# Second layer's prologue: first x from the residual's buffer, mask cast in two halves, second head's parts built inside unit 0

## The reference, cut to what matters

```python
h = maximum(layernorm(x), 0)
q = (h @ W).reshape(B, N, 4, 64)
e_src, e_dst = q @ a[:64], q @ a[64:]          # one number per node and head
e = leaky_relu(e_src[:, :, None] + e_dst[:, None], 0.2)
attn = softmax(where(adj > 0, e, -9e15), axis=2)
x = x + elu(attn @ q)
```

## Time and profile before

| | us |
|---|---|
| median of 3 runs | 5178.77 (5178.1 to 5178.99) |
| the profiled execution | 5176.52 |
| its span | 5174.7 |

### The profile page before, as it was taken

One profiled execution on the slowest core, in us unless ns is written; L12 is line 12 of the kernel. 1 busy time (PEld: TensorE's weight loads), 2 busy tenths in 40 slices (PEclk: granted clock), 3 DMA queues, 4 the chain that ended last, 5 costly groups with the idle time before them and its releaser, 6 DMA issues. The chain is left out here.

```text
span 5174.7 us, 139408 instructions
## 1 busy us (share of the span) xinstructions
PE 4889.2 (94%) x56608; PEld 4437.5 (86%) x56608; DVE 3751.2 (72%) x7147; ACT 2886.9 (56%) x3121; POOL 1364.6 (26%) x1472
## 2 busy tenths in 40 slices
PE   6999999999999999999999999993989989989999
PEld 5988888888898888888988889983989988989899
DVE  6666666666666666666666666664898898988898
ACT  4444444444444444444444444443878888878887
POOL 3343343334334333433433334331000000110100
PEclk9999999999999999999999999996999999999999
DMA  5000000000000000000000000003121121120210
GB/s 197 9 9 9 13 18 9 14 9 17 14 9 9 10 14 17 9 14 9 17 14 9 9 9 13 5 5 131 38 68 54 44 74 47 55 74 26 77 62 28
DMA packets 100064, 164.65 MB, mean 32 GB/s; under 512 B 5089, under 2 KB 91489, under 8 KB 92961
## 3 DMA queue, kind: packets, MB, share of 16 engines
q1 hardware_dynamic: 98464, 144.80, 8.4%
q0 software_dynamic: 896, 10.23, 0.5%
HBM read 112.79 MB, written 38.03 MB: 29 GB/s over the span
## 5 line engine op out<-in xcount | busy, mean ns | idle before, releaser
L551 PEld LDWEIGHTS outs<-v_s,probs 128*128 128x128 f32 x16384 | 1973.8, 192 | 81.7 <-issue 3.3
L551 PE MATMUL outs<-v_s,probs 128*128 128x128 f32 x16384 | 1984.0, 275 | 0.6 <-DVE probs L794 0.6
L654 ACT ACTIVATE slot<-slot,shift 128x1024 f32<-128x1024 f32 x1024 | 1111.3, 1088 | 1429.6 <-PE slot L541 1429.6
L794 DVE SCALAR_TENSOR_TENSOR probs<-slot,bound 128x1024 f32<-128x1024 f32 x1024 | 1250.9, 1224 | 723.1 <-ACT slot L654 720.1
L1354 ACT ACTIVATE cond<-s_all,d_sign 128x1024 bf16<-128x1024 f32 x1024 | 1123.7, 1142 | 196.9 <-DVE u L1509 191.7
L387 POOL TENSOR_TENSOR ctx_sum<-ctx_sum,ctx_part 128x256 f32<-128x256 f32 x896 | 646.6, 728 | 1267.3 <-DVE ctx_part L810 1266.5
L540 PE MATMUL slot<-q_hi,k_hl 128*128 128x512 f32 x2048 | 902.1, 441 | 1.0 <-DVE q_lo L750 1.0
L1255 PE MATMUL sums<-x_mixed,u 128*128 128x130 f16 x8192 | 807.1, 222 | 0.0
L1509 DVE TENSOR_TENSOR u<-cond,mask 128x1024 f16<-128x1024 bf16 x1024 | 694.6, 686 | 152.0 <-PE sums L1259 78.0
L541 PE MATMUL slot<-q_lo,k_hl 128*128 128x512 f32 x2048 | 802.1, 392 | 0.0
L1259 PE MATMUL sums<-x_mixed,mask 128*128 128x65 f16 x8192 | 778.6, 196 | 0.0
(11 more groups left out here) (135 smaller groups left out, 3820.6 us busy)
## 6 DMA issues: line engine op xcount, KB each, us to landing
s_all<-s_turned SPq DMA_DIRECT2D x32, 1024.0 KB, 4.9
xs<-in_x SPq DMA_DIRECT2D x32, 512.0 KB, 4.9
x<-y SPq DMA_DIRECT2D x32, 512.0 KB, 3.3
x_s<-x SPq DMA_DIRECT2D x32, 512.0 KB, 4.8
o_s<-x SPq DMA_DIRECT2D x16, 1024.0 KB, 6.1
out<-o_s SPq DMA_DIRECT2D x16, 1024.0 KB, 5.5
probs<-in_adj SPq DMA_DIRECT2D x11, 1024.0 KB, 5.3
bound<-in_adj SPq DMA_DIRECT2D x5, 1024.0 KB, 4.9
```

The source lines that it names most:

```text
L551: end = nc.tensor.matmul(outs[i % OUTS][:, q, :], probs[:, i % PROBS, r, q * P:(q + 1) * P], v_s[:, c * JC + r, h * E1:h * E1 + P], start= ...
L654: nc.scalar.activation(slot[:, :, :], slot[:, :, :], ACT.Exp, bias=shift[:, 0:1], scale=SCALE).then_inc(act_done, 1)
L794: nc.vector.scalar_tensor_tensor(probs[:, i % PROBS, :, :], spot(kind, "step", s, i)[:, :, :], P_LOW, bound[:, (i // H) % 2, :, :], ALU.ma ...
```

## The change

- SP loads x of batch 0 straight into `o_s`, in its two halves, as its first transfers after the weights; the four strip loads of batch 0 are gone. The statistics and normalize of batch 0 read `o_s`; normalize still writes `xs`, and from strip 2 on it waits until PE has transposed the strip that was in that buffer.
- The mask load leaves the head of POOL's stream. It now stands behind the constants and a wait on the second half of x, and it is two loads, one for each half of the columns. `inverse_std` for strip 0 stands behind both. DVE waits for a mask half at the start of unit 0 and of unit 1 of batch 0.
- `weigh`, `low` and `back` of head 1 of batch 0 move from the prologue into unit 0: `weigh` at steps 1 and 2, `low` at 6 and 7, `back` at 8; ACT's `high` of head 1 comes after `cond` of step 4.

```diff
-            def load_strip(pb, k, guard):
-                if guard:
-                    sp.wait_ge(pro_filled, t_use(pb, k, T_PAIRS - 1) - 2 * STRIP_PRO + 1)
+            def load_strip(pb, k):
+                sp.wait_ge(pro_filled, t_use(pb, k, T_PAIRS - 1) - 2 * STRIP_PRO + 1)
...
+            for half in range(HALVES):
+                load_res(0, half, False)
             for k in range(NS):
-                load_strip(0, k, k >= 2)
-                if k >= 2:
-                    store_s(0, k - 2)
-            store_s(0, NS - 2)
-            store_s(0, NS - 1)
+                store_s(0, k)
             spread_d(0)
             load_s(0, 0, False)
-
-            for half in range(HALVES):
-                load_res(0, half, False)
...
-            pool.dma_start(mask16[:, :, :], mask_dram).then_inc(mask_loaded, 16)
-            nc.gpsimd.memset(lift[:, :], LIFT)
...
+            pool.wait_ge(res_loaded[1], 16)
+            nc.gpsimd.memset(lift[:, :], LIFT)
+            for half in range(HALVES):
+                cols = slice(half * HALF, (half + 1) * HALF)
+                pool.dma_start(mask16[:, :, cols], mask_dram[:, :, cols]).then_inc(mask_loaded[half], 16)
...
             weights(0)
             high(0, 0, False)
-            high(0, 1, False)
...
+                        if first and m == 0 and j == 4:
+                            high(b, 1, False)
...
             def statistics(pb, k):
-                dve.wait_ge(x_loaded[k % 2], (pb * (NS // 2) + k // 2 + 1) * 16)
+                if isinstance(pb, int) and pb == 0:
+                    dve.wait_ge(res_loaded[k // 2], 16)
+                    src = o_s[:, k * IT:(k + 1) * IT, :]
+                else:
+                    dve.wait_ge(x_loaded[k % 2], ((pb - 1) * (NS // 2) + k // 2 + 1) * 16)
+                    src = xs[:, k % 2, :, :]
...
             def normalize(pb, k):
                 dve.wait_ge(rstd_done, pb * NS + k + 1)
+                src = xs[:, k % 2, :, :]
+                if isinstance(pb, int) and pb == 0:
+                    src = o_s[:, k * IT:(k + 1) * IT, :]
+                    if k >= 2:
+                        dve.wait_ge(pro_filled, t_use(0, k - 2, T_PAIRS - 1) + 1)
...
-            for h in range(2):
-                weigh(0, h, 0)
-                weigh(0, h, 1)
-                low(0, h, 0)
-                low(0, h, 1)
-                back(0, h)
-            dve.wait_ge(mask_loaded, 16)
+            weigh(0, 0, 0)
+            weigh(0, 0, 1)
+            low(0, 0, 0)
+            low(0, 0, 1)
+            back(0, 0)
...
+                    if first and m < HALVES:
+                        dve.wait_ge(mask_loaded[m], 16)
...
+                        if first and m == 0:
+                            if j in (1, 2):
+                                weigh(b, 1, j - 1)
+                            if j in (6, 7):
+                                low(b, 1, j - 6)
+                            if j == 8:
+                                back(b, 1)
```

More of the change, by code:

```diff
@@ L1022, in layer1_block @@
         ones_ready = sem("ones_ready")
-        mask_loaded = sem("mask_loaded")
+        mask_loaded = [sem("mask_loaded0"), sem("mask_loaded1")]
         x_loaded = [sem("x1_loaded0"), sem("x1_loaded1")]
@@ L1146, in batch @@
                     if m < NS and not last:
-                        load_strip(b + 1, m, True)
+                        load_strip(b + 1, m)
                     if m < HALVES and not first:
@@ L1428, in statistics @@
             def statistics(pb, k):
-                dve.wait_ge(x_loaded[k % 2], (pb * (NS // 2) + k // 2 + 1) * 16)
+                if isinstance(pb, int) and pb == 0:
[4 more added lines that the diff above has]
+                    src = xs[:, k % 2, :, :]
                 for t in range(IT):
-                    last = nc.vector.bn_stats(stats[:, t, :], xs[:, k % 2, t, :])
+                    last = nc.vector.bn_stats(stats[:, t, :], src[:, t, :])
                 last.then_inc(stats_done, 1)
@@ L1442, in normalize @@
                 dve.wait_ge(rstd_done, pb * NS + k + 1)
+                src = xs[:, k % 2, :, :]
[3 more added lines that the diff above has]
+                        dve.wait_ge(pro_filled, t_use(0, k - 2, T_PAIRS - 1) + 1)
                 for t in range(IT):
-                    last = nc.vector.tensor_scalar(xs[:, k % 2, t, :], xs[:, k % 2, t, :], moments[:, t, 0:1], rstd[:, t:t + 1],
+                    last = nc.vector.tensor_scalar(xs[:, k % 2, t, :], src[:, t, :], moments[:, t, 0:1], rstd[:, t:t + 1],
                                                    ALU.subtract, ALU.mult)
```

## The result

| | us |
|---|---|
| kernel before, median of 7 runs | 5178.1 (5174.12 to 5182.56) |
| changed kernel, median of 7 runs | 5160.92 (5153.08 to 5162.7) |
| ratio, with its 95% interval | 0.9965 (0.9956 to 0.9974) |
| profiled execution of the changed kernel, span | 5162.7, 5160.9 |

The change makes the kernel 17 us faster, a third of a per cent. The forecast was 5161.3. That agreement is partly luck: the stage up to unit 1 gained 3 us more than forecast, and the time after it gave back about as much. One of the executions of e8 further down ran at a granted clock of 0.842 and took 5604.86 us; its ratio leaves that one out.

The account below looks back on a forecast made before the run. At the layer seam DVE stands 16.84 us for a_s behind the mask, everything else behind DVE. Terms 11.4 + 0.6 + 7.27 - 1.75 = 17.5 us, taken from 5178.8, give 5161.3; range 5153.5 to 5169.

Parts of the forecast that it names:

- part 3: Strips of batch 0: still 5.85 us apart; small stores hardly feel the moved mask, 0 (0 to 2 us lost).
- Part 1: Seam start, x ahead of the mask: DVE folds at 3518.2, ready for strip 0's rstd 16.9 us earlier.
- Part 2: POOL before strip 0's rstd: x wait and two mask issues of 3.28 us leave 11.4 us gained (16.9 to -7).
- rival A: POOL's mask issues nearly free, about 0.6 us per half: rstd moves 16.9, total gain 23.0 us, 5155.8; chance 0.18.
- the likeliest case: The main forecast, with 3.28 us of POOL's time per mask half: 5157 to 5166, chance 0.60.
- Rivals B: POOL held back by the DMA engines at the mask issue, free between 3535 and 3547: 5168 to 5180; chance 0.12.
- D: At POOL's mask issue each run costs a fixed 6 ns or more: slower, 5191 at 9 ns; chance 0.05.
- Part 4: Spread through memory: faster without the residual's 2 MB just behind it in the queue, 0.6 us gained (0 to 1.3).
- Part 5: Head 1's parts moved into unit 0: first pick 7.27 us earlier, unit 0 longer by 1.75 (0 to 7.2).
- the walk: Stepping through unit 0 on the old clock: DVE waits 1.5 us for ACT's cond 5, later conds early.
- Rival C: Unit 0 starves PE, whose clock stays low longer, costing 5 to 8 us: 5168; chance 0.05.
- The lead should reach the end: After the seam, order and work are unchanged, so the 17.5 us should last; failing if unit 2's lead differs at the end.

Follow-up runs that it names:

- e8: Changed kernel with ACT's high of head 1 behind cond 5 of unit 0 instead of cond 4; ratio 0.9964, median 5160.17 us.
- e4: Changed kernel with both mask halves issued first in POOL's stream, without the wait for x; ratio 0.9966, median 5157.98 us.
- e7: Kernel before with only the mask load cut into two halves, still first in POOL's stream; ratio 0.9984, median 5168.92 us.
- a2_after: Changed kernel run again, unaltered, beside its variants on one chip; ratio 0.9967, median 5162.27 us.
- e5: Changed kernel with both mask loads behind POOL's rstd of strip 0 instead of ahead of it; ratio 0.9965, median 5157.34 us.
- e3: Changed kernel with the mask in one load instead of two halves, still behind x; ratio 0.9966, median 5154.99 us.
- e2: Kernel before with only head 1's parts moved from the prologue into unit 0; ratio 0.9996, median 5169.2 us.
- e9: Changed kernel with two idle fills on DVE ahead of the first pick; ratio 0.9967, median 5159.02 us.
- e10: Changed kernel with five idle fills on DVE ahead of the first pick; ratio 0.9971, median 5159.48 us.

## Why the prediction was right, step by step

**What bounded the kernel:** right in place, incomplete in cause. DVE stood for a_s and everything stood behind DVE; with that gone the seam is 14.4 us shorter up to rstd (27.55 to 13.16). But I called the cause "the mask first", and part 3 used its rows of 64 KB only to argue that stores would be safe. e4 and e7 show that issuing the mask first need not hold a_s and x up. In two pieces it starts 1 us later, behind nearly all of a_s, and its rows of 2 KB then let x through in turns. The halves alone (e7) bring rstd to 12.32, with the mask still first.

**Part 1** held: fold at 3518.10 for 3518.2, statistics at 3521.13 and moments in time for 3523.

**Part 2 is the term that was mis-sized.** Forecast: x's second half at 3522.0, 3.28 us for each mask half, POOL free at 3528.6, 11.4 gained. Measured: 3523.5, 1.22 each, 3525.99, and 14.4 gained from w_s on (14.0 from the start of the span). The 4.1 us less for the issue came from the slope in the earlier trace rows, 1.4 ns for a run. From one run per partition (0.547) to sixteen (1.22) it is 0.35 ns for a run; the step from one to two runs does not extend. Here the Trainium skill's sentence in "DMA: Bandwidth & Descriptors", Anatomy of one DMA, that many descriptors can be emitted before the cost shows, was nearer to the trace than the slope, though 1.22 is not 0.55. The mechanism of this term was nearer to rival A's 0.6 than to the 3.28 of the likeliest case; the gain up to rstd came half way between the two, 11.4 and 16.9, because x's second half landed 1.5 later than forecast. Rivals B and D are excluded by the same rows: POOL did not wait for the engines.

**Part 3:** the strips kept 5.85, and the spread did not meet the mask. The stores of strip 0 did: with rows of 2 KB they were to feel it hardly, and they waited 6.7 us for their first packet. The term of 0 held because ACT wants them 11.5 us after their issue, as the prediction also says. What came besides was 1.0 us in strip 0, between rstd and its last product (10.95 before, 9.96 here, 10.26 in a2_after, 12.4 in e5): PE's clock came up earlier or later in it. It differs between two traces of one kernel (9.96 and 10.26), and I had given it no width.

**Part 4 was wrong.** From PE's last product of strip 3 to DVE's reduce it is 8.96 us before and 8.85 after, and the row above: 0.1, not 0.6. The residual's loads behind the spread went, but others moved up into their place (s_all's second half and x of the next batch, issued within 3.2 us of it). So the runs do not tell whether transfers behind it make it long.

**Part 5** held: 7.27 at the first pick (3572.43 for back to 3572.80 for the pick, nothing between), and unit 0 of 23.58 for 23.2. The wait at cond 5 that the walk found is there, 1.34 for 1.5, under PE's name. Rival C did not happen in unit 0, where PE's clock was up sooner than before (0.85 for the unit against 0.82). A milder form of it happened in unit 1, which took 27.52 where I had "about 26", 1.5 us more, at a place where PE had just waited 2.08 us for DVE. The same wait stands in unit 1 of every trace, the kernel before too, and in e3 the clock stayed up. Of the ten traces with part 5 six have the low clock in unit 1 (both of the changed kernel, e2, e4, e9, e10), of the four without it none. What part 5 adds ahead of it is a wait of PE of 1.48 us near the end of unit 0; that this leads to the low clock is not shown. PE's timeline, the changed kernel first, then e3 (the same 32 products each):

```profile
3617.36 1.76 PE L1247 MATMUL sums<-x_plain,u 128*128 128x65 f16 x32 [2.08 <-DVE u L1525]
```

```profile
3615.45 1.19 PE L1245 MATMUL sums<-x_plain,u 128*128 128x65 f16 x32 [2.08 <-DVE u L1523]
```

**The sum.** Forecast lead at unit 1: 17.5. Measured: 20.6 from w_s, which is 3.0 more in part 2, 0.5 more between rstd and the first pick (1.0 from the clock, 0.5 less from part 4), and 0.4 less in unit 0. Of that, 17.2 us came out in the medians and 13.8 in the spans of the two profiled executions. "The lead should reach the end" holds over all the kernels together (0.92), not for the profiled pair: its lead was 19.1 at unit 2 and 14.3 at the end, both from w_s, which the prediction had named as a sign that it fails. The low clock takes or gives some us in any one pair (116 against 92 us of it here), and 5161.3 met 5160.92 because an underestimate of 3 in front stood against such a loss behind.

## What to carry to other kernels

A wide cast with long contiguous rows makes other queues pay one of its rows for each of theirs. Cut it into rows of a few KB (2 KB here, for 1.8 us more of POOL's time to issue it), and see which small transfer (here 64 KB of weights) everything waits for. Issue that one so that its packets are ahead of the cast's first, since a transfer issued into the stream of 2 KB rows still waited 6.7 to 6.8 us for its first packet (e7, changed kernel). A load that is moved behind a wait on an engine's stream takes that engine's next work with it; put it behind the first urgent instruction, not ahead (e5: rstd 3.8 us sooner, of which 1.4 reached unit 1). For edits of a few us, read stages counted from a common event, and keep the clock's scatter in the range of the total.

## What was not expected of the hardware

A transfer of 8 rows of 512 B per DMA engine took 22.1 us beside a cast with rows of 64 KB. With the cast in two pieces, issued at the same place, the cast's first packet came 1.0 us later and the same transfer took 3.6 us, ahead of it. Beside rows of 2 KB a load of 512 KB took 11.8 us where it takes 3.7 alone, 6.8 of them before its first packet. Four stores of 2 KB needed 14 us beside rows of 64 KB and 8.4 beside rows of 2 KB; their first packet started 6.6 and 6.7 us after the issue. Issuing a load of 2048 runs cost POOL 1.22 us, of 128 runs 0.55 to 0.66. Two traced executions of one kernel repeat their stages up to unit 1 within 0.5 us. Over all of its executions the changed kernel's time differs by 10 us (5153.08 to 5162.7), for a mean granted clock of 0.985 against 0.982; over the runs of all kernels 0.001 of mean clock goes with 3.5 us.
